# A decoder layer on one core: q through an SBUF stage with its heads innermost, ternary transfers issued by GpSimd, and a new order at the start and between the phases

## The reference

```python
# attention over heads, for each token by itself (n = token, 32 half-heads of 16)
q = split_qk(x @ Wq.T) * 512 ** -0.5;  k = split_qk(x @ Wk.T);  v = x @ Wv.T     # 16 heads of 32
att = softmax(einsum('bnqd,bnkd->bnqk', q, k))                 # 32 x 32 for each token
lam = exp(sum(lq1 * lk1)) - exp(sum(lq2 * lk2)) + LAM_INIT
diff = att[:, :, :16, :16] - lam * att[:, :, 16:, 16:]
o = einsum('bnah,bhnd->bnad', diff, v);  o = o * rsqrt(mean(o * o) + eps) * (1 - LAM_INIT)
x = layernorm(x + o @ Wo.T + bo)
# cross part: r_t = decay * r_(t-1) + ctx_t * ctx_t along the sequence
x = layernorm(x + x * r)
# feed-forward with ternary weights (groups of 64: sign, threshold and mean magnitude)
h = relu(x @ w1.T) ** 2;  x = layernorm(x + rms_norm(h) @ w2.T)
```

## Time and profile before

| | |
|---|---|
| profiled execution | 1160.84 us, span 1159.0 us |
| busy: TensorE, VectorE, ScalarE, GpSimd | 1042.1 (90%), 926.5 (80%), 565.7 (49%), 243.5 (21%) us |
| chain that ended last | TensorE 64%, VectorE 20%, ScalarE 5%, transfers 3% |
| first projection, first up-projection | 9.63 us, 556.93 us |
| transfers | 165,671 packets, 139.71 MB, of them 139,872 under 512 B |
| transfers, median from issue to landing | k 8.0 us, qbd 4.2, q's write 3.8, w 5.2 |
| copy `f_sb<-ps_f` 128x512 on ScalarE (L788) | x64, mean 599 ns |
| granted clock, in 40 slices | full but for the slices near 60 us, 460 to 500 us and 520 to 580 us, where it is 3 to 8 tenths |

### The profile page before, as it was taken

One profiled execution on the slowest core, in us unless ns is written; L12 is line 12 of the kernel. 1 busy time (PEld: TensorE's weight loads), 2 busy tenths in 40 slices (PEclk: granted clock), 3 DMA queues, 4 the chain that ended last, 5 costly groups with the idle time before them and its releaser, 6 DMA issues.

```text
span 1159.0 us, 20344 instructions
## 1 busy us (share of the span) xinstructions
PE 1042.1 (90%) x6992; PEld 825.5 (71%) x7008; DVE 926.5 (80%) x1668; ACT 565.7 (49%) x866; POOL 243.5 (21%) x237
## 2 busy tenths in 40 slices
PE   6799999899998998443799999999999999999994
PEld 5577676676776776333688888888888888888883
DVE  4368888888888999968678797997979969789555
ACT  5323333343433342310656666575665675656672
POOL 5211252525252525050602002020020010200000
PEclk9899999999999999666799999999999999999997
DMA  7967696859596868786321311412114113100010
GB/s 279 279 159 174 141 239 142 238 140 241 140 244 143 205 148 203 199 239 227 122 42 37 74 37 36 109 36 67 42 36 109 36 34 74 37 34 4 1 37 36
DMA packets 165671, 139.71 MB, mean 121 GB/s; under 512 B 139872, under 2 KB 139872, under 8 KB 159456
## 3 DMA queue, kind: packets, MB, share of 16 engines
q1 hardware_dynamic: 94432, 113.57, 35.8%
q10 hardware_dynamic: 71168, 25.17, 8.6%
HBM read 82.09 MB, written 52.43 MB: 116 GB/s over the span
## 4 chain that ended last, share of the span: by engine, by line
PE 64%; DVE 20%; ACT 5%; issue 4%; DMA 3%; SPq 2%; POOL 1%; ACTq 1%; DVEq 0%; POOLq 0%
PE ps_f L670 20%; PE ps_s L686 19%; PE ps_f L533 9%; PE ps_o L621 7%; PE ps_s L550 5%; DVE row_sum L1012 2%; DVE sc L995 1%; DVE row_max L998 1%; DVE st L989 1%; SPq L389 1%; DVE o_sb L1045 1%; PE ps_f L621 1%; DVE st L1023 1%; DVE sc L993 1%; DVE xtl L961 1%
## 5 line engine op out<-in xcount | busy, mean ns | idle before, releaser
L670 PE MATMUL ps_f<-x2h,w 128*128 128x512 f32 x512 | 204.8, 400 | 1.6 <-DVE x2l L1193 1.6
L670 PE MATMUL ps_f<-x2l,w 128*128 128x512 f32 x512 | 201.4, 393 | 0.0
L686 PE MATMUL ps_s<-w,hh 128*128 128x512 f32 x500 | 196.6, 393 | 0.0
L686 PE MATMUL ps_s<-w,hl 128*128 128x512 f32 x500 | 194.9, 390 | 0.0
L533 PE MATMUL ps_f<-xth,wh 128*128 128x512 f32 x384 | 159.4, 415 | 12.9 <-DVE xtl L961 9.6
L1201 DVE TENSOR_TENSOR hl<-h_sb,hh 128x512 fp32r<-128x512 f32 x128 | 95.5, 746 | 94.5 <-ACT hh L885 94.4
L533 PE MATMUL ps_f<-xtl,wh 128*128 128x512 f32 x384 | 150.6, 392 | 0.0
L533 PE MATMUL ps_f<-xth,wl 128*128 128x512 f32 x384 | 150.6, 392 | 0.0
L550 PE MATMUL ps_s<-qbd,k 128*32 128x128 f32 x2048 | 125.1, 411 | 17.7 <-DMA qbd<-q_scr 17.4
L1391 POOL TENSOR_TENSOR xb<-xb,bob 128x512 f32<-128x512 f32 x32 | 47.4, 1512 | 430.5 <-DMA xb<-in_x 430.5
L550 PEld LDWEIGHTS ps_s<-qbd,k 128*32 128x32 f32 x2048 | 83.4, 147 | 54.1 <-DMA qbd<-q_scr 15.4
(11 more groups left out here) (134 smaller groups left out, 1807.1 us busy)
## 6 DMA issues: line engine op xcount, KB each, us to landing
x_raw<-in_x_turned SPq DMA_DIRECT2D x8, 1024.0 KB, 7.5
q_scr<-f_sb ACTq DMA_DIRECT2D x32, 256.0 KB, 3.8
k_scr<-f_sb ACTq DMA_DIRECT2D x32, 256.0 KB, 2.6
w_scr<-w_in SPq DMA_DIRECT2D x16, 512.0 KB, 5.2
v_scr<-f_sb ACTq DMA_DIRECT2D x32, 256.0 KB, 5.6
k<-k_scr SPq DMA_DIRECT2D x8, 1024.0 KB, 8.0
qbd<-q_scr SPq DMA_DIRECT2D x128, 64.0 KB, 4.2
v<-v_scr SPq DMA_DIRECT2D x64, 128.0 KB, 5.6
```

Of the source, the lines that this page charges most:

```text
L670: last = nc.tensor.matmul(ps_f[:, j % 2, :], w1[:, j // 2, k, (j % 2) * P:(j % 2 + 1) * P], xx[:, k, :], start=(k == 0 and xx is x2h), sto ...
L686: last = nc.tensor.matmul(ps_s[:, t, :], a[:, j % 4, t * P:(t + 1) * P], w2[:, j, :], start=(j == 0 and a is hh), stop=(j == HC - 1 and a ...
```

## The change

- **q.** `q_scr` gets k's layout with the token lane outside (two halves), so q is written in pieces of 64 tokens as k is. One transfer for each half brings it to `q_stage` (in the place of the other tile's `xth`), ScalarE turns it there so that the heads are innermost (`q_turn`, four copies a tile), and eight transfers copy the lanes from SBUF to SBUF into `qbd`, which is now [2 halves of groups, lanes, groups, heads]. `scores` reads `qbd[:, c % 2, :, j * 8 + gq, :]`.
- **Ternary weights.** Their loads and writes leave SyncE's order and are issued by GpSimd.
- **Columns and lanes.** The host sorts x's tokens otherwise within a tile (`lanes_apart`), v's copies read PSUM with a step of 4, and `v2_load` is one transfer.
- **Order in phase one.** Scores at n = 0, 1, 5, 7; the third exponential before copy 8; the next x parts at n = 9; o written a body later; k after qbd; wo written last in body 0. Bodies 2 and 3 are written out.
- **Start.** The first weights and x come in four parts each, and the first two projections go part by part (`project_first`).
- **Passage.** The first tile's split and output projections are done before the softmax of tile 7 ends, with four banks; the last mix's turning, squares and scaling move into body 0 of phase two.

```diff
     def lane_slot(t):
-    return (t % 4) * 2 + t // 4
+    return (t // 2 % 2) * 4 + t // 4 * 2 + t % 2
-    q_scr = nc.dram_tensor("q_scr", [NSB, D, SB], F32, kind="Internal").ap()
+    q_scr = nc.dram_tensor("q_scr", [NSB, 2, LANES, D // 2, G], F32, kind="Internal").ap()
+        q_stage = sb("x", "q_stage", [P, 2, 2, H * G], F32)     # same place as xth
-        qbd = sb("y", "qbd", [P, LANES, H, G], F32)
+        qbd = sb("y", "qbd", [P, 2, LANES, G // 2, H], F32)
-        AT_SCORES = (0, 1, 6, 8)
+        AT_SCORES = (0, 1, 5, 7)
-        AT_SUMS = (4, 5, 10, 10)
+        AT_SUMS = (4, 5, 10, 11)
         def proj_bank(i, t):
-            return ps_o[:] if later(i) else ps_f[:, t % 2, :]
+            return ps_o[:] if later(i) else (ps_f[:, 0, :], ps_f[:, 1, :], ps_t[:], ps_o[:])[t]
...
+            def q_load(i, s, place):
+                sp.dma_start(q_in(place), q_scr[i, s].rearrange("t (d a) g -> (t d) a g", a=H)).then_inc(qin_ld, 16)
+            def qbd_load(place):
+                for t in range(LANES):
+                    sp.dma_start(qbd[H * t:H * (t + 1), :, lane_slot(t), :, :],
+                                 q_turned(place)[H * t:H * (t + 1)]).then_inc(qbd_ld, 16)
+            def first_half_load(i, place):
+                hold(*([(s_ps, at(i, 16, 0))] if later(i) else [(zeroed, 2), (wtr_lo, 12)]), (q_tn, at(i, 4, 2)))
+                qbd_load(place)
+            def second_half_load(i, place):
+                hold((q_tn, at(i, 4, 4)), (s_ps, at(i, 16, 8)))
+                qbd_load(place)
...
             def body(i, par, do_2, do_1):                       # SyncE
+                if do_1:
+                    second_half_in(i - 1, 1 - par)
                 if later(i) and not (isinstance(i, int) and i == NSB - 1):
                     x_load(i + 1, 1 - par)
+                if do_2 and not (isinstance(i, int) and i == 2):
+                    o_write(i - 3)
                 if do_2:
                     dbd_load(i - 2)
-                if later(i):
-                    w_write(i - 1, 1)
-                    w_load(i, 0)
                 if do_1:
-                    second_half_load(i - 1)
+                    second_half_load(i - 1, 1 - par)
+                first_half_in(i, 1 - par)
                 if do_1:
                     v2_load(i - 1)
-                w_write(i, 0)
-                w_load(i, 1)
+                first_half_load(i, 1 - par)
+                k2_load(i)
                 if not later(i):
                     wo_write()
-                first_half_load(i)
-                if do_2:
-                    o_write(i - 2)
...
             def x_upper(i, par, k):                             # ScalarE
+                if k == 0 and later(i):
+                    act.wait_ge(qbd_ld, at(i - 1, 256, 128))
...
+            def q_turn(i, c, place):
+                gh = c % 2
+                if gh == 0:
+                    act.wait_ge(qin_ld, at(i, 32, 16 * (c // 2 + 1)))
+                    if c or later(i):
+                        act.wait_ge(qbd_ld, at(i, 256, 128 * (c // 2)))
+                nc.scalar.activation(q_turned(place)[:, gh, :, :].rearrange("p (j g) a -> p j g a", j=4),
+                                     q_in(place).rearrange("p a (h g j) -> p h j g a", j=4, h=2)[:, gh, :, :, :],
+                                     ACT.Copy).then_inc(q_tn, 1)
...
             def body(i, par, do_2, do_1):
                 for n in range(12):
+                    if do_1 and n == 8:
+                        exps(i - 1, 2)
                     f_copy(i, n)
-                    if do_1 and n in (1, 3, 8, 11):
-                        exps(i - 1, (1, 3, 8, 11).index(n))
+                    if do_1 and n in (1, 3):
+                        exps(i - 1, n // 2)
+                    if do_1 and n == 11:
+                        exps(i - 1, 3)
+                    if do_1 and n == 1:
+                        q_turn(i - 1, 2, 1 - par)
+                        q_turn(i - 1, 3, 1 - par)
+                    if n == 5:
+                        q_turn(i, 0, 1 - par)
+                        q_turn(i, 1, 1 - par)
-                    if n == 7 and not (isinstance(i, int) and i == NSB - 1):
+                    if n == 9 and not (isinstance(i, int) and i == NSB - 1):
                         for k in range(KC):
                             x_upper(i + 1, 1 - par, k)
...
+            soft_first(NSB - 1, 2)                              # VectorE, passage
             mixed_turn(NSB - 2, 3)
+            out_lower(0)
...
             diff_turn(NSB - 1)
-            out_lower(0)
             for t in range(TT):
                 add_projection(0, t)
+            scan(0, range(KC))
             x1_norm(0)
-            scan(0, range(KC))
-            mixed_turn(NSB - 1, 0)
-            mixed_turn(NSB - 1, 1)
             for t in range(TT):
                 add_scan(0, t)
...
             def body(i, par, do_2, do_1):                       # GpSimd
                 w_ternary(i, 0)
+                w_write(i, 0)
+                w_load(i, 1)
...
                 w_ternary(i, 1)
+                w_write(i, 1)
+                if not (isinstance(i, int) and i == NSB - 1):
+                    w_load(i + 1, 0)
+            w_load(0, 0)
             phase_a(pool, body)
```

214 lines of the change are left out of this document (124 added, 90 removed).

## The result

The changed kernel took 1194.55 us (median of 4 runs, 1191.21 to 1195.76), the kernel before on the same chip 1163.11 (1158.12 to 1166.39): a ratio of 1.027, 95% interval 1.0225 to 1.0314. The forecast was 1117. The profiled execution has a span of 1190.4 us, 31.4 more than before.

The account below looks back on a forecast made before the run. The prediction took VectorE's pace to bound phase one's steady loop and TensorE phase two. Gains of 15.4 + 8 + 0.7 + 15.5 + 4.5 = 44 us from 1160.84 gave 1117, range 1093 to 1137.

Parts of the forecast that it names:

- Scores in 2.1 us: Phase one, TensorE: 64 score instructions fall from 3.88 to 2.1 us once q is read with heads inside.
- The steady bodies: Phase one's loop, paced by VectorE: five bodies gain 1.4 us each and the last 1.0, 8 us in all.
- Net -1.4 a body: Steady body: VectorE waits removed (-0.9 and -1.5) against a new x parts wait (+1.0); ends -5 and +3.
- the second rival: Steady bodies: GpSimd's issues make |w| late or stretch VectorE's operations, 2 us a body more, giving 1133; chance 0.2.
- Start and first body: Kernel start to first `dt`: softmax 13.2 us earlier plus 2.2 from the body's other waits, 15.4 us gained.
- the absolute value comes near 20.5: Start, ScalarE: GpSimd's first ternary load issues at 16.0 us, so the absolute value comes near 20.5 instead of 21.4.
- No one else waits for it, so nothing: Steady body: TensorE waits up to 3.5 us for copies and |w| queued on ScalarE, but its idle 10 us absorb it.
- The passage: From `dt` 7 to the end of x2n, 44.4 us: output projections and other work move away, gaining 15.5 us; bounds 10 and 16.
- the slip that the forecast named: Passage: the last mix, needing dbd, ends 15 us after `dt`, VectorE wants transposes at 16.6; 15.5 taken for a small slip.
- First body of phase two: Feed-forward's first body: xb's bias going first gives 5.5 us, moved-in work costs 1, gain 4.5.
- The first, all of VectorE's waits falling: Steady bodies at VectorE's floor: 5 us a body gained rather than 1.4, 68 us in all, giving 1093; chance 0.15.
- The third, the x parts' wait: Each phase-one body: next x parts wait for qbd's landing; landing at S + 16 gives 1171, slower than before; chance 0.06.

Follow-up runs that it names:

- e5: Changed kernel with k's groups stored apart, so successive score matmuls read k 64 bytes apart instead of 4; 1167.1 us, ratio 1.0027 to the kernel before.
- e1: Changed kernel with the ternary loads and writes issued by SyncE again at their old places; 1184.6 us, ratio 1.021 to the kernel before.
- e15: e14 with the change's order of the steady body (scores, sums, third exponential, next x parts); 1166.2 us, ratio 1.0021 to the kernel before.
- e16: e14 with the change's order of scores, sums and exponentials, the next x parts left at their old place; 1163.1 us, ratio 0.9999.
- e9: e5 with q's stage in room of its own (v's low weight part left out), so x parts wait for no q; 1164.7 us.
- e18: e9 with e10's late o write and the steady body's order as in the kernel before; 1154.1 us, ratio 0.9908 to the kernel before.
- e2: Kernel before with GpSimd issuing the ternary loads and writes, and bodies 2 and 3 written out; 1177.3 us, ratio 1.014.
- e6: e5 with the ternary loads and writes issued by SyncE again at their old places; 1165.1 us, ratio 1.0021 to the kernel before.
- e13: Kernel before with the change's passage alone and the last mixed tile's write behind the third attention tile's loads; 1153.0 us, ratio 0.9921.
- e10: e5 with the write of the last mixed tile issued behind the third attention tile's loads; 1163.0 us, ratio 0.9996 to the kernel before.
- e14: e13 with the wo write behind the first k and q loads in body 0; 1145.51 us, ratio 0.987 to the kernel before.
- e3: Changed kernel with q loaded straight into qbd, without stage or turning copies, scores reading with a step of 64 elements; 1342.5 us, ratio 1.156.
- e7: Kernel before with one index changed, so successive score matmuls read words 4 bytes apart in k2 and qbd; 1353.4 us, single run.

## Why the prediction was wrong

**Scores in 2.1 us: right** (2.08). That they come off a TensorE with time to spare: right too, and so worth nothing in itself.

**The steady bodies: wrong by 40 us over six of them, the largest miss.** The step that failed is "Net -1.4 a body". It added up VectorE's waits and took its busy time as given. The waits behaved (15.8 us in four bodies for 18.2), and the busy time rose by 6 us in the body shown. The six bodies together took 378.1 us; 337.7 was forecast. Shown: e5, which moves only k's groups, takes 20 of the 40 back (358.2); e1 gives 1.6 a body to GpSimd's issues in the changed kernel, which I had put at 0; e15 and e16 give the order the wrong sign where scores take 3.9 us. Without the wait (e9) the six take 357.0, with the old order as well (e18) 353.3. Not settled: that is still 7.6 above the kernel before (345.7). e2, which adds GpSimd's issues to that kernel and writes two bodies out, stands 7.7 above it, so they are large enough to be the rest; but e6 takes them out of e5 and gains nothing, and no run takes them out of e18. The 8 us of gain appear in no run.

**GpSimd's issues, the second rival, at 1133:** its direction was right. By its place among the rivals it would be 2 us a body; it is 0.7 a body, 3.8 in the sixth and 5.6 at the start on the kernel before (e2). Its argument, that both engines stretch each other's work, explains the smaller part of the stretching. The larger part lies beside scores and hits ScalarE as well. But sum what VectorE's instructions that meet no scores and run beside one of GpSimd's take over the lower quartile of their kind, in the four bodies: 13.4 us in the changed kernel, 5.8 in e1, 7.0 before, 12.2 in e2. GpSimd's scaling of the heads stands in its program behind the transfers' waits and so falls on other instructions of VectorE: before, it runs beside the subtraction of the row maximum (2.2 us there for 1.2); in e5 beside the next x parts (6.1 us too long in four bodies, 0 in e6).

**Start and first body: wrong by 23 us** ("First `dt`: 13.2 + 2.2 = 15.4 us earlier"; it came 8.0 later). The first matmul came 2.8 us earlier (6.86 for 9.63), where I took 4, and then the step "the absolute value comes near 20.5" failed. ScalarE's queue and transfer issue after:

```profile
19.43 5.49 ACTq L837 DMA_DIRECT2D q_scr<-f_sb  x1
26.58 1.06 ACT L865 ACTIVATE w_b<-w_in 128x1024 bf16<-128x1024 f32 x1 [0.97 <-DMA w_in<-in_fc_turned]
50.03 2.19 ACT L812 ACTIVATE xth<-x_raw 128x512 fp32r<-128x512 f32 x4 [4.47 <-DMA qbd<-q_stage]
52.13 1.04 ACT L865 ACTIVATE w_b<-w_in 128x1024 bf16<-128x1024 f32 x1
```

The ternary load, issued by GpSimd at 15.96, landed 10.6 us later, and one write's issue held ScalarE 5.5 us (0.37 for the write before it). TensorE's waits until the first `dt`, after:

```profile
PE ps_t L605 <- ACT w_b L865: 11.8, 3, 5.6
PE ps_f L614 <- DVE xtl L1023: 6.9, 1, 6.9
PE ps_f L551 <- ACT f_sb L827: 3.0, 3, 1.2
PE ps_s L568 <- DMA qbd<-q_stage: 2.8, 1, 2.8
```

Up to here TensorE sets the pace, and 11.8 us of waits for the absolute value are more than the 8.4 that the wo write gave back. "No one else waits for it, so nothing" was said of the steady body and carried over to body 0, where it doesn't hold. Loading from SyncE instead does not cure it by itself (e6: 9.4 us). The neighbours stretch the first bodies as well; with a scatter of 7 us at this place their share can't be told.

**The passage: right** (-16.0 for -15.5), and independent of what precedes it only in part: e13 gains 11.6 there of the 16. Of the other 4.4, 2.9 are the slip that the forecast named: in e13 TensorE stands 16.3 us for the last mix's `dbd` (9.2 in the changed kernel), and VectorE then waits 2.9 us for the scan's transposes. The other 1.5 are its scans, which take 6.8 us for 5.3.

**First body of phase two: wrong by 12 us** (+7.2 for -4.5; the body itself, `x2n` to `x2n`, takes 77.4 us, 69.8 before). "Gain 4.5" rested on TensorE's 3.68 us behind xb being the bias's. In e5 the bias was long done and TensorE still stood 3.74 there, since VectorE reaches that addition only after ScalarE's queue, which had taken the last mix's squares. The loads behind the late write add 3.2 (e10). In e10 this body is still 3.5 us longer than before; which of the turnings, sums and squares moved in costs that, no run shows.

**The other rivals.** The first, all of VectorE's waits falling, did not come: 15.8 of 18.2 us stayed. The third, the x parts' wait, was the only road to a slower kernel that I priced, at 6%. It was there, and with the neighbours gone it was worth no more than the scatter (e9). The 6% were given to "slower" for a reason that did not bring it about. The one that came true was in no case: an index inside a matmul's operand, in a part of the change that I had read only for its step.

## What to carry to other kernels

Before costing a new order of small matmuls, write down the addresses that successive ones read: 4 bytes apart they slowed themselves and the engines beside them here, 64 bytes apart they did not, and nothing between was tried. When an engine's busy time grows at equal work, sort its longest instructions by what each other engine ran at that moment, before blaming transfers. And a placement tuned to one duration (scores of 3.9 us) may hold for that duration only; take it apart from the change that shortens them, as e14 and e15 do.

## What was not expected of the hardware

Score matmuls of 32 columns stationary and 128 moving in fp32, 64 in a row: 3.9 us with a step of 256 bytes in the moving operand and successive ones 64 bytes apart; 7 to 8 us with both operands of successive ones 4 bytes apart; 6.1 to 7.4 with only the moving one near; 2.1 to 2.2 with the moving one read 16 neighbours at a time and the stationary one near; 1.9 to 2.0 so with neither near. These are at the full granted clock. At 0.50 the stepped ones took 3.92 all the same; at 0.53, from 83.76 us in the changed kernel, the short ones took 3.63. With both operands near VectorE, ScalarE and GpSimd hold an instruction until about the scores' end, up to 8.4 us for one of 0.6 to 1.7. The Trainium skill (SBUF - State Buffer, the section on the two separate sides) has it that within the engine side only the pair of ports that VectorE and GpSimd share causes contention, and that ScalarE and TensorE wait for no one. The traces of e3 and e7 disagree: in e3 ScalarE's copy took 7.47 us for 0.60 beside scores, with nothing being transferred from 468 us on. Theory D as recorded names the port of a bank; what it is that the engines meet at, no run shows.
